# Moving the gates' bias product behind the expert loop, and pacing nine expert weight loads from GpSimd, in a one-core graph layer

## The chip, the cores and the metric

One core of one Trainium2 chip runs the whole layer as a single hand-ordered program: five engines with a program each, and semaphores between them. The metric is the device time of that core in microseconds, the median of several runs. The profile is of one further execution, whose own time is given beside it.

## The reference, cut to what matters

1250 nodes of 512 features pass through a graph convolution, an attention-like mixer and then a layer of 16 experts, of which each node uses its two best. Only the last part is touched by the change:

```python
logits = xt @ router_w.T + router_b
probs = softmax(logits)
topk_p, topk_i = top_k(probs, 2)
gates = sum(one_hot(topk_i) * topk_p)          # 1250 x 16
for e in range(16):
    h = gelu(xt @ w1[e].T + b1[e])             # 512 -> 256
    y = h @ w2[e].T + b2[e]                    # 256 -> 512
    out += y * gates[:, e]
x = x + out
```

The second bias is separable: the sum over the experts of gate times b2 is one product, gates (1250 x 16) by b2 (16 x 512). The kernel computes it so.

## The kernel before, in words

The nodes are cut into 10 tiles of 128 rows (the last has 98). FC_TILES groups them into 3, 3, 2 and 2. For each group the kernel makes the graph part's hidden and output products, normalises, and routes. Routing gives each (node, choice) a row ("slot") in a DRAM table `xs`, where every expert owns its own stretch.

What follows the last group, in order:

- GpSimd scatters the normalised rows into `xs`: 20 indirect DMAs, two per tile (L569). The last four belong to the last group and can start only when its slots are known (`slots_ready`).
- VectorE works out the tile table (`te`, `lies_at`, `tbase`, `npair`: which expert and which rows each 128-row tile of slots has) and then raises `route_ready`.
- ScalarE issues eight expert weight loads back to back (experts 1 to 8, L695) as soon as the last output product (`mix_ps`) is done. Each is 1 MB: 128 rows of 8 KB. SyncE has loaded experts 0 and 15 long before, and loads 9, 10, 11 just before the last routing.
- TensorE turns the gates of every tile (L1303, into bank 0 or 1), ScalarE copies them out (L700, `gt_saved`), TensorE multiplies them by b2 (L1309, into bank 2 or 3, `gb_ps`), and VectorE adds the result to `xr` (L1016, `gb_added`). Product t waits for the addition of t-2, since there are two banks.
- SyncE waits for all scatters (L400) and loads the first two tiles of slots, `xg[0]` and `xg[1]` (L402). TensorE turns them (`turn_rows`, L1315), ScalarE copies them (L704). SyncE then loads tiles 2 and 3 (L405), and the last three experts 12, 13, 14.
- The expert loop handles two tiles per turn. TensorE: first products (L1333), turning of the next two tiles (L1315), second products (L1346). ScalarE: Gelu (L714) and copies of turned rows (L720). VectorE copies the next tile's first weights into `w1_now` (L1026, after `w_ready` has counted its expert), and results out of PSUM (L1038). SyncE stores the results (L417) and loads the next slots (L414). TensorE reads the turn count and four table entries into registers (L1323, L1325, L1326) before each turn's first product (L1333).
- GpSimd counts the experts in order into `w_ready` (L575), and after the loop gathers both results of each node (L585). VectorE adds them with their gates (L1043, L1045), and SyncE stores the output (L422).

The order of instructions on an engine is the order of the text; a wait holds back everything behind it on its engine.

Of the kernel before, what the change touches and what calls it, by code (L numbers as in the profile page):

```python
# [23 lines left out]
P = 128  # L24
N = 1250
D = 512
NT = 10
# [6 lines left out]
FC_TILES = [range(0, 3), range(3, 6), range(6, 8), range(8, 10)]  # L34
# [20 lines left out]
EXP = 16  # L55
DFF = 256
KF = DFF // P
EW = KD * DFF + KF * D
# [10 lines left out]
def layer(nc, x, src, dst, wqkv, wo, bo, gw1, gb1, gw2, gb2, geps, rw, rb, ew, eb1, eb2, out):  # L69
    f32r = mybir.dt.float32r  # L70
    f32, f16, bf16, i32 = mybir.dt.float32, mybir.dt.float16, mybir.dt.bfloat16, mybir.dt.int32
    ALU = mybir.AluOpType
# [5 lines left out]
    with ExitStack() as ctx:  # L78
# [10 lines left out]
        arena = sb("arena", [P, SLAB // 4])  # L89
# [75 lines left out]
        xr = at(VT + NT * D * 4, [NT, D])  # L165
# [18 lines left out]
        logits, prob, tmp, oh1, oh2, rank, gates = (small(k, NT, EXP) for k in range(7))  # L184
# [7 lines left out]
        gates_t = at(S + 14336, [NT * P], parts=EXP)  # L192
        w1_now = at(S + 19456, [2, KD * DFF])

        ident = sb("ident", [P, P])
# [25 lines left out]
        b2_sb = sb("b2_sb", [EXP, D])  # L221
# [15 lines left out]
        bank = [ctx.enter_context(nc.psum_tensor(f"bank{i}", [P, 512], f32)) for i in range(8)]  # L237
# [8 lines left out]
        ew_in = [sem(f"ew_in{e}") for e in range(EXP)]  # L246
# [24 lines left out]
        mix_ps, x2_ready = sem("mix_ps"), sem("x2_ready")  # L271
# [19 lines left out]
        def rows(t):  # L291
            return LAST if t == NT - 1 else P
# [48 lines left out]
        def _(sp):  # L341
# [37 lines left out]
            def expert(e):  # L379
                sp.dma_start(arena[:, expert_at(e):expert_at(e) + EW], ew[e]).then_inc(ew_in[e], 16)  # L380
# [23 lines left out]
                sp.wait_ge(xgt_ps[a], 1)  # L404
                sp.dma_start(xg[:, a, :], rows_of(2 + a)).then_inc(xg_in[a], 16)  # L405

            for e in (12, 13, 14):
                expert(e)
            n = sp.value_load(npair[0:1, 0:1], min_val=1, max_val=(MAXT - 3) // 2)
            with sp.Fori(0, n) as j:  # L410
                for a in range(2):
# [14 lines left out]
        def _(pool):  # L426
# [139 lines left out]
            for t in range(NT):  # L566
                pool.wait_ge(slots_ready, 1 + sum(1 for tiles in FC_TILES if tiles[-1] < t))
                for k in range(2):
                    pool.indirect_dma_start(  # L569
                        out=xs, out_offset=bass.IndirectOffsetOnAxis(ap=slot[0:rows(t), k, t:t + 1], axis=0),  # L570
                        in_=x2n[0:rows(t), t, :], in_offset=None).then_inc(scattered, 16)

            for e in range(EXP):
                pool.wait_ge(ew_in[e], 16)
                pool.sem_inc(w_ready, 1)  # L575

            pool.wait_ge(route_ready, 1)
            n = pool.value_load(npair[0:1, 0:1], min_val=1, max_val=(MAXT - 3) // 2)
# [12 lines left out]
        def _(act):  # L591
# [99 lines left out]
                    act.activation(x2n_t[:, t % 2, :, :], bank[6][:, :].rearrange("p (k n) -> p k n", k=KD),  # L691
                                   copy).then_inc(x2nt_saved, 1)
            act.wait_ge(mix_ps, NT)
            for e in range(1, 9):
                act.dma_start(arena[:, expert_at(e):expert_at(e) + EW], ew[e]).then_inc(ew_in[e], 16)  # L695
            exponents(len(FC_TILES) - 1)

            for t in range(NT):
                act.wait_ge(gt_ps, t + 1)
                act.activation(gates_t[:, t * P:(t + 1) * P], bank[t % 2][0:EXP, 0:P], copy).then_inc(gt_saved, 1)  # L700

            for a in range(2):
                act.wait_ge(xgt_ps[a], 1)
                act.activation(xg_t[:, a, :, :], bank[4 + a][:, :].rearrange("p (k n) -> p k n", k=KD),  # L704
                               copy).then_inc(xgt_saved[a], 1)
            act.wait_ge(eb1_in, 16)
            act.wait_ge(route_ready, 1)
            n = act.value_load(npair[0:1, 0:1], min_val=1, max_val=(MAXT - 3) // 2)
# [15 lines left out]
        def _(dve):  # L724
# [285 lines left out]
            dve.sem_inc(route_ready, 1)  # L1010
            weigh(len(FC_TILES) - 1)

            for t in range(NT):
                r = rows(t)
                dve.wait_ge(gb_ps, t + 1)
                dve.tensor_tensor(xr[0:r, t, :], xr[0:r, t, :], bank[2 + t % 2][0:r, :], ALU.add).then_inc(gb_added, 1)  # L1016


            for a in range(2):
                dve.sem_inc(y_saved[a], 1)  # L1020
                dve.sem_inc(y_stored[a], 16)
# [17 lines left out]

            for t in range(NT):  # L1040
                r = rows(t)
                dve.wait_ge(yg_in[t], 32)
                link(dve.scalar_tensor_tensor(out=xr[0:r, t, :], in0=yg[0:r, 0, t, :], scalar=gate[0:r, 0, t:t + 1],  # L1043
                                              in1=xr[0:r, t, :], op0=ALU.mult, op1=ALU.add))
                dve.scalar_tensor_tensor(out=xr[0:r, t, :], in0=yg[0:r, 1, t, :], scalar=gate[0:r, 1, t:t + 1],  # L1045
                                         in1=xr[0:r, t, :], op0=ALU.mult, op1=ALU.add).then_inc(res_ready, 1)

        @block.tensor
        def _(pe):
# [244 lines left out]
            route(NT - 1)  # L1294
            ranks(len(FC_TILES) - 1)

            pe.wait_ge(b2_in, 16)
            for f, tiles in enumerate(FC_TILES):
                pe.wait_ge(gates_ready, f + 1)
                for t in tiles:  # L1300
                    if t >= 2:
                        pe.wait_ge(gt_saved, t - 1)
                    pe.transpose(bank[t % 2][0:EXP, 0:P], gates[:, t, :], ident[:, :]).then_inc(gt_ps, 1)  # L1303
                for t in tiles:
                    r = rows(t)
                    pe.wait_ge(gt_saved, t + 1)
                    if t >= 2:
                        pe.wait_ge(gb_added, t - 1)
                    pe.matmul(bank[2 + t % 2][0:r, :], gates_t[:, t * P:t * P + r], b2_sb[:, :],  # L1309
                              start=True, stop=True).then_inc(gb_ps, 1)  # L1310


            def turn_rows(a):
                for k in range(KD):
                    ins = pe.transpose(bank[4 + a][:, k * P:(k + 1) * P], xg[:, a, k * P:(k + 1) * P], ident[:, :])  # L1315
                ins.then_inc(xgt_ps[a], 1)

            pe.wait_ge(x2_ready, NT)
            for a in range(2):
                pe.wait_ge(xg_in[a], 16)  # L1320
                turn_rows(a)
            pe.wait_ge(route_ready, 1)
            n = pe.value_load(npair[0:1, 0:1], min_val=1, max_val=(MAXT - 3) // 2)  # L1323
            with pe.Fori(0, n) as j:
                e = [pe.value_load(te[0:1, bass.ds(2 * j + a, 1)], min_val=0, max_val=EXP - 1) for a in range(2)]  # L1325
                lies = [pe.value_load(lies_at[0:1, bass.ds(2 * j + a, 1)], min_val=expert_at(EXP - 1),  # L1326
                                      max_val=expert_at(0)) for a in range(2)]
                for a in range(2):
                    pe.wait_ge(w1_ready[a], j + 1)
                    pe.wait_ge(xgt_saved[a], j + 1)  # L1330
                    for m in range(KF):
                        for k in range(KD):
                            ins = pe.matmul(bank[a][:, m * P:(m + 1) * P],  # L1333
                                            w1_now[:, a, k * DFF + m * P:k * DFF + m * P + P],
                                            xg_t[:, a, k, :], start=(k == 0), stop=(k == KD - 1),
                                            skip_group_check=True)
                    ins.then_inc(h_ps[a], 1)
                for a in range(2):
                    pe.wait_ge(xg_in[a], 16 * (j + 2))
                    turn_rows(a)  # L1340
                for a in range(2):
                    pe.wait_ge(w_ready, e[a] + 1)
                    pe.wait_ge(hg_ready[a], j + 1)
                    pe.wait_ge(y_saved[a], j + 1)
                    for k in range(KF):
                        ins = pe.matmul(bank[6 + a][:, :], hg_t[:, a, k, :],  # L1346
                                        arena[:, bass.ds(lies[a] + KD * DFF + k * D, D)],
                                        start=(k == 0), stop=(k == KF - 1))
                    ins.then_inc(y_ps[a], 1)


# [29 lines left out]
```

## Time and profile before

| | |
|---|---|
| median of 3 runs | 878.91 us (877.94 to 879.23) |
| profiled execution, its own time | 879.67 us |
| span of the profile | 877.5 us |
| TensorE matmul busy | 775.1 us (88%) |
| VectorE, ScalarE, GpSimd busy | 521.7, 281.1, 155.3 us |
| mean granted TensorE clock | 0.942 |

Times in the rows are microseconds from the span's start. The granted clock is given as a share of full speed: 1.00 is 2.4 GHz and 0.50 is 1.2 GHz. "PEld" is TensorE's weight load, "SPq", "ACTq", "PEldq" the instruction sequencer of an engine. The work around the change lies between 676 us (last output product) and the end.

### The profile page before, as it was taken

The page shows a single profiled execution, that of the slowest core. Times are in us where ns is not written, and L with a number is a line of the kernel's source. Part 1 is how long each engine was busy: PE and PEld are TensorE (multiplying, and loading weights), DVE is VectorE, ACT ScalarE, POOL GpSimd, SP SyncE. Part 2 cuts the span into 40 slices and gives each one's busy share as a digit, 9 for nine tenths or more (in the row PEclk, how much of TensorE's full clock was granted, in tenths as well). Part 3 has the DMA queues.
Part 4 walks back from the last instruction along what each step waited for, and adds up shares of the span by engine and source line. Part 5 has one row for each costly group of instructions (what it writes and reads, how often), then busy time and mean ns, then how long its engine had stood idle before and what let it go on. Part 6 is the DMA issues. An engine that isn't in the chain of part 4 may idle for free.

```text
span 877.5 us, 11469 instructions
## 1 busy us (share of the span) xinstructions
PE 775.1 (88%) x3351; PEld 517.9 (59%) x3352; DVE 521.7 (59%) x1494; ACT 281.1 (32%) x578; POOL 155.3 (18%) x198
## 2 busy tenths in 40 slices
PE   4999998989989998979799999999998599999910
PEld 2555443666756676656577744677887256766700
DVE  4563336798989989898877534435445523333234
ACT  2212111352534444343345402323333123434300
POOL 5040003022130403040400042002021100000045
PEclk9999999999999999999799999999999559999965
DMA  9126000807162526253351091001015945343357
GB/s 296 8 44 241 1 0 1 295 1 251 46 210 87 182 104 198 98 160 137 105 191 49 1 357 47 1 0 72 1 73 192 377 184 187 109 135 114 131 163 235
DMA packets 48071, 111.61 MB, mean 127 GB/s; under 512 B 7066, under 2 KB 7082, under 8 KB 45584
## 3 DMA queue, kind: packets, MB, share of 16 engines
q1 hardware_dynamic: 43248, 91.41, 30.8%
q0 software_dynamic: 3616, 11.17, 4.0%
q10 hardware_dynamic: 1152, 8.39, 2.4%
q8 instruction: 24, 0.39, 0.2%
q14 instruction: 31, 0.25, 0.1%
HBM read 44.73 MB, written 58.54 MB: 118 GB/s over the span
## 4 chain that ended last, share of the span: by engine, by line
PE 70%; DVE 20%; issue 4%; POOL 2%; DMA 2%; ACT 2%; SPq 0%; DVEq 0%; POOLq 0%
PE bank L1110 8%; PE bank L1141 7%; PE bank L1272 7%; DVE arena L825 6%; PE bank L1218 6%; PE bank L1333 6%; PE bank L1169 6%; DVE p_lo L861 6%; PE bank L1346 5%; PE bank L1081 4%; PE bank L1152 4%; PE bank L1203 4%; DVE arena L827 3%; PE bank L1188 3%; PE bank L1185 3%
## 5 line engine op out<-in xcount | busy, mean ns | idle before, releaser
L657 ACT ACTIVATE p_hi<-bank 128x416 fp32r<-128x416 f32 (+1 forms) x240 | 123.8, 518 | 201.2 <-PE bank L1169 199.7
L861 DVE SCALAR_TENSOR_TENSOR p_lo<-bank,p_hi 128x416 fp32r<-128x416 f32 (+1 forms) x240 | 140.2, 586 | 40.7 <-ACT p_hi L657 39.7
L825 DVE TENSOR_SCALAR arena<-iota,arena 125x128 f16<-125x128 f16 x392 | 137.9, 352 | 37.0 <-PE bank L1081 34.8
L827 DVE TENSOR_SCALAR arena<-iota,arena 125x320 f16<-125x320 f16 x392 | 115.7, 295 | 0.0
L1169 PE MATMUL bank<-q_hi,k_hl 128*128 128x416 f32 (+1 forms) x240 | 114.9, 479 | 0.1
L1188 PE MATMUL bank<-p_lo,v_hl 128*128 128x416 f32 (+1 forms) x240 | 91.0, 379 | 21.6 <-DVE p_lo L861 21.2
L1110 PE MATMUL bank<-arena 128*128 128x512 f32 x200 | 103.0, 597 | 0.8 <-ACT arena L618 0.8
L1081 PE MATMUL bank<-arena 125*128 125x320 f16 x392 | 96.7, 311 | 5.8 <-issue 3.5
L1185 PE MATMUL bank<-p_hi,v_hl 128*128 128x416 f32 (+1 forms) x240 | 86.5, 360 | 0.0
L1169 PE MATMUL bank<-q_lo,k_hl 128*128 128x416 f32 (+1 forms) x240 | 86.1, 359 | 0.0
L1081 PEld LDWEIGHTS bank<-arena 125*128 125x128 f16 x392 | 34.4, 100 | 75.7 <-issue 53.2
L1141 PE MATMUL bank<-arena 128*128 128x416 f32 (+1 forms) x192 | 73.1, 529 | 2.1 <-ACT arena L600 2.1
L1272 PE MATMUL bank<-arena 128*128 128x384 f32 (+2 forms) x256 | 70.3, 430 | 0.0
L1188 PEld LDWEIGHTS bank<-p_lo,v_hl 128*128 128x128 f32 x240 | 46.6, 194 | 35.2 <-DVE p_lo L861 34.1
L1333 PEld LDWEIGHTS bank<-arena 128*128 128x128 f32 x448 | 53.0, 198 | 17.4 <-issue 16.0
L1333 PE MATMUL bank<-arena 128*128 128x128 f32 x448 | 55.3, 283 | 6.6 <-issue 5.6
L1026 DVE COPY arena<-arena 128x1024 f32 x30 | 20.8, 695 | 67.3 <-issue 67.3
L1169 PEld LDWEIGHTS bank<-q_hi,k_hl 128*128 128x128 f32 x240 | 47.1, 196 | 20.2 <-issue 13.5
L1272 PEld LDWEIGHTS bank<-arena 128*128 128x128 f32 x256 | 47.7, 190 | 17.6 <-issue 0.5
L1141 PEld LDWEIGHTS bank<-arena 128*128 128x128 f32 x192 | 36.2, 195 | 29.7 <-issue 26.3
L509 POOL COPY arena<-arena 125x20 f32 (+1 forms) x40 | 8.5, 212 | 246.8 <-DVE arena L827 207.5
L1346 PE MATMUL bank<-arena 128*128 x112 | 50.4, 592 | 0.0
(208 smaller groups left out, 1018.9 us busy)
## 6 DMA issues: line engine op xcount, KB each, us to landing
slots<-arena SPq DMA_DIRECT2D x6, 5376.0 KB, 19.3
slots<-arena SPq DMA_DIRECT2D x2, 5120.0 KB, 19.0
arena<-in_ew SPq DMA_DIRECT2D x8, 1024.0 KB, 10.7
arena<-in_ew ACTq DMA_DIRECT2D x8, 1024.0 KB, 13.2
arena<-slots SPq DMA_DIRECT2D x32, 256.0 KB, 2.8
slots<-arena SPq DMA_DIRECT2D x28, 256.0 KB, 2.1
arena<-in_gw SPq DMA_DIRECT2D x2, 2048.0 KB, 16.7
arena<-in_wqkv SPq DMA_DIRECT2D x3, 1024.0 KB, 14.2
```

Source lines behind the costliest of these rows:

```text
L657: act.activation(p_hi[0:kt, s % NPB, 0:n], bank[s % NQB][0:kt, 0:n], ACT.Relu).then_inc(p_hi_ready, 1)
L825: dve.tensor_scalar(ring[:, at_slot:at_slot + P], iota16[0:CE, 0:P], window_cols[:, i % WBUF, 1, k:k + 1], None, ALU.is_equal)
L827: dve.tensor_scalar(ring[:, at_slot + P:at_slot + OHW], iota16[0:CE, :], window_cols[:, i % WBUF, 0, k:k + 1], None, ALU.is_equal).then_in ...
L861: dve.scalar_tensor_tensor(out=p_lo[0:kt, s % NPB, 0:n], in0=bank[s % NQB][0:kt, 0:n], scalar=0.0, in1=p_hi[0:kt, s % NPB, 0:n].bitcast(f3 ...
L1081: return pe.matmul(bank[AW[w % 2]][:, 0:WCOL], of[:, at_slot:at_slot + P], of[:, at_slot + P:at_slot + OHW], start=start, stop=stop, skip_ ...
L1110: ins = pe.matmul(bank[NB][:, :], a_t[:, g % 2, t, :], xn[:, t, :], start=(t == 0), stop=(t == NT - 1))
L1141: ins = pe.matmul(bank[g % 5][:, 0:n], w_qkv[:, k, c:c + P], xn_t[:, k, o:o + n], start=(k == 0), stop=(k == KD - 1))
L1169: ins = pe.matmul(bank[s % NQB][0:kt, 0:n], k_hl[h % 2][:, t * P:t * P + kt], q[h % 2][:, o:o + n], start=first, stop=not first)
L1185: pe.matmul(bank[AV + m % 2][:, 0:n], v_hl[0:kt, t, h, :, :], p_hi[0:kt, s % NPB, 0:n], start=(t == 0), stop=False)
L1188: pe.matmul(bank[AV + m % 2][:, 0:n], v_hl[0:kt, t, h, :, :], p_lo[0:kt, s % NPB, 0:n], start=False, stop=(t == NT - 1)).then_inc(av_step, 1)
L1272: ins = pe.matmul(bank[g % 4][:, 0:n], w1[:, k, m * P:(m + 1) * P], rst_t[:, k, o:o + n], start=(k == 0), stop=(k == KD - 1))
L1333: ins = pe.matmul(bank[a][:, m * P:(m + 1) * P], w1_now[:, a, k * DFF + m * P:k * DFF + m * P + P], xg_t[:, a, k, :], start=(k == 0), stop ...
```

## The change

It has three parts, and it keeps what is computed.

1. The ten gate-by-bias products move behind the expert loop on TensorE, and the ten additions into the tail on VectorE, one ahead of each tile's two final additions. The turning of the gates stays before the loop: eight tiles ahead of `turn_rows`, the last two behind it; TensorE then waits until all ten are copied.
2. ScalarE issues only experts 1 and 2; SyncE no longer issues 12, 13 and 14.
3. GpSimd, after the scatters, waits until `xg[1]` has landed, and then issues 3, 4, 5, 6, 7, 8, 12, 13, 14: two at first and one more each time the next expert from number 3 on has been counted.

```diff
-            for e in (12, 13, 14):          # SyncE, after the loads of tiles 2 and 3
-                expert(e)
...
+            pool.wait_ge(xg_in[1], 16)      # GpSimd, after the scatters
+            pool.wait_ge(mix_ps, NT)
+            late = [3, 4, 5, 6, 7, 8, 12, 13, 14]
+
+            def load_next():
+                e = late.pop(0)
+                pool.dma_start(arena[:, expert_at(e):expert_at(e) + EW], ew[e]).then_inc(ew_in[e], 16)
+
+            load_next()
+            load_next()
             for e in range(EXP):
                 pool.wait_ge(ew_in[e], 16)
                 pool.sem_inc(w_ready, 1)
+                if e >= 3 and late:
+                    load_next()
...
-            for e in range(1, 9):           # ScalarE
+            for e in range(1, 3):
                 act.dma_start(arena[:, expert_at(e):expert_at(e) + EW], ew[e]).then_inc(ew_in[e], 16)
...
-            for t in range(NT):             # VectorE, before the loop
-                r = rows(t)
-                dve.wait_ge(gb_ps, t + 1)
-                dve.tensor_tensor(xr[0:r, t, :], xr[0:r, t, :], bank[2 + t % 2][0:r, :], ALU.add).then_inc(gb_added, 1)
...
             for t in range(NT):             # VectorE, after the loop
                 r = rows(t)
+                dve.wait_ge(gb_ps, t + 1)
+                link(dve.tensor_tensor(xr[0:r, t, :], xr[0:r, t, :], bank[2 + t % 2][0:r, :], ALU.add))
+                dve.sem_inc(gb_added, 1)
                 dve.wait_ge(yg_in[t], 32)
...
+            for f in range(len(FC_TILES) - 1):      # TensorE, before the loop
+                turn_gates(f)
             pe.wait_ge(x2_ready, NT)
             for a in range(2):
                 pe.wait_ge(xg_in[a], 16)
                 turn_rows(a)
+            turn_gates(len(FC_TILES) - 1)
+            pe.wait_ge(gt_saved, NT)
             pe.wait_ge(route_ready, 1)
...
+            pe.wait_ge(b2_in, 16)           # TensorE, after the loop
+            for t in range(NT):
+                r = rows(t)
+                if t >= 2:
+                    pe.wait_ge(gb_added, t - 1)
+                pe.matmul(bank[2 + t % 2][0:r, :], gates_t[:, t * P:t * P + r], b2_sb[:, :],
+                          start=True, stop=True).then_inc(gb_ps, 1)
```

(The words behind # in the diff name the engine; they are not in the code.) ScalarE's copies follow TensorE's order: gates of tiles 0 to 7, both `xg` copies, gates of tiles 8 and 9.

## Rows read from the trace of the kernel before

**Rows 1.** Busy time of each engine by stretch, with granted clock and DMA.
```profile
core 0: us, PE busy (x) PEld busy (x) DVE busy (x) ACT busy (x) POOL busy (x), PEclk, DMA share, GB/s
686.00:696.00 10.00, 4.91 (x15) 1.57 (x15) 8.45 (x33) 0.90 (x4) 4.38 (x4) 0.50 1.01 410
696.00:705.00 9.00, 8.43 (x12) 2.56 (x13) 2.96 (x6) 0.74 (x3) 0.00 (x0) 0.50 1.01 420
718.00:724.00 6.00, 6.00 (x38) 5.57 (x38) 0.82 (x2) 3.30 (x7) 0.00 (x0) 0.77 0.98 374
```

**Rows 2.** The chain that ended last, from routing into the loop: start, us, what.
```profile
693.94 0.12 DVE tbase L1008
...
710.05 3.79 PE bank L1309 x4
...
716.74 5.74 PE bank L1333 x32
...
727.41 3.81 PE bank L1333 x32
```

**Rows 3.** Instructions in order of time, last scatter to first loop turn.
```profile
692.21 1.32 POOL L569 DMA_INDIRECT slots<-arena,slot  x1 [0.30 <-issue]
...
709.42 0.69 DVE L1016 TENSOR_TENSOR arena<-arena,bank 128x512 f32<-128x512 f32 x1 [1.02 <-PE bank L1309]
709.73 0.48 ACT L700 ACTIVATE arena<-bank 16x128 f32<-16x128 f32 x2 [3.97 <-PE bank L1303]
...
713.76 1.97 PE L1315 MATMUL bank<-ident,arena 128*128 128x128 f32 x8
...
714.91 0.60 ACT L704 ACTIVATE arena<-bank 128x512 f32<-128x512 f32 x1 [4.70 <-PE bank L1315]
```

**Rows 4.** Single lines: the wait for the scatters, and landing times (L695, L402, L405).
```profile
L400 SPq EVENT_SEMAPHORE  x1: 17/17/17, 701.3 to 701.3; - x1
...
L695 ACTq DMA_DIRECT2D arena<-in_ew x8: 393/468/738, 680.4 to 684.1; - x8
...
DMA to landing us min/median/max: 5.1/13.2/21.5
...
L402 SPq DMA_DIRECT2D arena<-slots x2: 343/350/357, 702.4 to 703.5; - x2
...
DMA to landing us min/median/max: 3.6/3.8/3.9
...
DMA to landing us min/median/max: 2.8/2.8/2.8
```

**Rows 5.** Single lines: what TensorE's sequencer does between its last wait and the first turn.
```profile
L1323 PEldq TENSOR_LOAD <-npair x1: 307/307/307, 710.4 to 710.4; - x1
...
L1329 PEldq ALU_OP  x14: 32/32/32, 714.2 to 829.6; - x14
```

**Rows 6.** Single lines: landing of loop loads (L414), loop stores (L417), gathers (L585).
```profile
DMA to landing us min/median/max: 2.5/2.7/5.9
...
DMA to landing us min/median/max: 2.0/2.1/4.3
...
DMA to landing us min/median/max: 3.3/4.1/5.0
```

**Rows 7.** Instructions in order of time: GpSimd's first plain loads, at the span's start.
```profile
2.92 0.76 POOL L441 DMA_DIRECT2D arena<-in_dst  x1 [0.73 <-POOL ident L438]
```

**Rows 8.** Instructions in order of time: an addition beside a scatter, and the tail.
```profile
643.02 0.96 POOL L569 DMA_INDIRECT slots<-arena,slot  x1 [0.30 <-issue]
...
643.31 0.69 DVE L976 TENSOR_TENSOR arena<-arena,bank 128x512 f32<-128x512 f32 x1 [0.96 <-PE bank L1218]
...
847.45 0.75 DVE L1043 SCALAR_TENSOR_TENSOR arena<-arena,gate 128x512 f32<-128x512 f32 x1 [8.78 <-DMA arena<-slots,slot]
...
850.58 1.42 POOL L585 DMA_INDIRECT arena<-slots,slot  x1 [0.30 <-issue]
...
873.27 0.75 DVE L1043 SCALAR_TENSOR_TENSOR arena<-arena,gate 98x512 f32<-98x512 f32 x1 [1.26 <-DMA arena<-slots,slot]
```

More of the change, by code:

```diff
@@ L693, in _ @@
             act.wait_ge(mix_ps, NT)
-            for e in range(1, 9):
+            for e in range(1, 3):
                 act.dma_start(arena[:, expert_at(e):expert_at(e) + EW], ew[e]).then_inc(ew_in[e], 16)
             exponents(len(FC_TILES) - 1)
-            for t in range(NT):
-                act.wait_ge(gt_ps, t + 1)
-                act.activation(gates_t[:, t * P:(t + 1) * P], bank[t % 2][0:EXP, 0:P], copy).then_inc(gt_saved, 1)
+            for tiles in FC_TILES[:-1]:
+                for t in tiles:
+                    act.wait_ge(gt_ps, t + 1)
+                    act.activation(gates_t[:, t * P:(t + 1) * P], bank[t % 2][0:EXP, 0:P], copy).then_inc(gt_saved, 1)
             for a in range(2):
@@ L705, in _ @@
                                copy).then_inc(xgt_saved[a], 1)
+            for t in FC_TILES[-1]:
+                act.wait_ge(gt_ps, t + 1)
+                act.activation(gates_t[:, t * P:(t + 1) * P], bank[t % 2][0:EXP, 0:P], copy).then_inc(gt_saved, 1)
             act.wait_ge(eb1_in, 16)
@@ L1011, in _ @@
             weigh(len(FC_TILES) - 1)
-            for t in range(NT):
-                r = rows(t)
-                dve.wait_ge(gb_ps, t + 1)
-                dve.tensor_tensor(xr[0:r, t, :], xr[0:r, t, :], bank[2 + t % 2][0:r, :], ALU.add).then_inc(gb_added, 1)
             for a in range(2):
@@ L1295, in _ @@
             ranks(len(FC_TILES) - 1)
[L1297 to L1310, printed above, removed]
             def turn_rows(a):
@@ L1316, in turn_rows, with turn_gates @@
                 ins.then_inc(xgt_ps[a], 1)
+            def turn_gates(f):
+                pe.wait_ge(gates_ready, f + 1)
+                for t in FC_TILES[f]:
+                    if t >= 2:
+                        pe.wait_ge(gt_saved, t - 1)
+                    pe.transpose(bank[t % 2][0:EXP, 0:P], gates[:, t, :], ident[:, :]).then_inc(gt_ps, 1)
+            for f in range(len(FC_TILES) - 1):
+                turn_gates(f)
             pe.wait_ge(x2_ready, NT)
@@ L1349, in _ @@
                     ins.then_inc(y_ps[a], 1)
+            pe.wait_ge(b2_in, 16)
+            for t in range(NT):
+                r = rows(t)
+                if t >= 2:
+                    pe.wait_ge(gb_added, t - 1)
+                pe.matmul(bank[2 + t % 2][0:r, :], gates_t[:, t * P:t * P + r], b2_sb[:, :],
+                          start=True, stop=True).then_inc(gb_ps, 1)
 def kernel(x, src, dst, L0_gnn_W1, L0_gnn_b1, L0_gnn_W2, L0_gnn_b2, L0_gnn_eps, L0_mix_W_qkv, L0_mix_W_out,
```

## The prediction

> **What bounds the kernel now.** I read the chain of waits first, then busy time by stretch, then single lines. The reader should look only at what lies between the end of routing and the first turn of the expert loop. The tile table is ready at 694.1 (693.94 + 0.12) [rows 2], and the loop's first product starts at 716.74 [rows 2]: 22.7 us in which the chain is nearly all L1309, the gate-by-bias products, with L1303 and L1016 between them. They run at a granted clock of 0.50 (1.2 GHz) [rows 1].
>
> A second path runs beside this one and is shorter. From 686 to 705 the DMA engines are full (share 1.01, 410 to 420 GB/s) [rows 1]: that is ScalarE's eight weight loads, issued from 680.4 to 684.1 and landing up to 21.5 us later [rows 4]. The last scatter is issued at 692.21 [rows 3], but the wait for all scatters ends only at 701.3 [rows 4], and the two slot loads go out at 702.4 and 703.5 and take 3.6 to 3.9 us [rows 4]. So the second tile has landed at about 703.5 + 3.6 = 707.1. Taking the products away alone would leave this path; the change attacks both.
>
> **Part 1, the products leave.** Ten products, ten additions and their waits go from the stretch 695.5 to 713.8. Nothing needs them before the tail. What is late next is `xg[1]`.
>
> **Part 2, the scatters and slot loads meet empty DMA engines.** Only experts 1 and 2 are in flight from 680.4, 2 MB, which at the smallest landing time of such a load, 5.1 us [rows 4], are gone by 687. The last scatter starts at about 692.1 as now (it hangs on `slots_ready`, not on DMA). It then needs 3.3 to 5.0 us to land, by the gathers of the same engine and size [rows 6], the nearest rows; I take 4.0, so 696.1. Now it takes 701.3 - 692.2 = 9.1. SyncE needs 1.1 us from the wait to its first load (701.3 to 702.4) and 1.1 more to the second [rows 4]: issue at 698.3. A load of this kind with little beside it takes 2.8 us (the lower of the two landings of slot loads) [rows 4]. `xg[1]` lands at 701.1, between 700.4 and 702.1.
>
> Here a row shows how queues share. Four scatters, 1.05 MB in 2 KB rows, start at 688.2 and are all landed at 701.3 [rows 4], that is 80 GB/s, while the total is 410 to 420 [rows 1]. That is 2 parts in 10, as 2 KB stand to 2 + 8 KB. The Trainium skill says in "DMA: Bandwidth & Descriptors", section "Queues, rings and completion order", that each DMA engine goes round the rings that have work, a packet of descriptors at a time. By that rule the trace agrees (80 of 420); if the queues were served first come, first served instead, the scatters would have had to wait for nearly all of the loads, to about 684.1 + 21.5 = 705.6 [rows 4].
>
> **From `xg[1]` to the first product.** TensorE turns the tile: half of 1.97 us [rows 3], 1.0. ScalarE starts 0.15 later and copies it in 0.60, then copies the gates of tiles 8 and 9 in 0.48 [rows 3]. With 0.2 for hand-overs, `gt_saved` is complete at 701.1 + 0.1 + 1.0 + 0.15 + 0.6 + 0.5 + 0.1 = 703.55. This wait is new, and behind it on TensorE stand the reads of `npair`, two entries of `te` and two of `lies_at` into registers. Now they start at 710.4, right after the addition of 709.42 + 0.69 that releases the last product's wait, and end at 714.2 [rows 3, 5]: 3.9 us, hidden today under products and turnings that TensorE still had queued. With the change nothing covers them. The first product starts at about 703.55 + 3.95 = 707.5.
>
> The other inputs are earlier. GpSimd, which before counted `w_ready` freely, now waits for `xg[1]`, then issues two loads. Its plain loads take 0.76 us or less [rows 7], so it counts at about 702.7, and VectorE's copy (L1026) ends at 703.6. The queued work behind GpSimd's wait is only this counting. It stays 3.9 us clear of TensorE.
>
> The start moves from 716.74 to 707.5: -9.2 us (-10.8 to -8.0 by the ends above and half a microsecond of hand-overs).
>
> **Part 3, the first turn.** Its 32 products take 5.74 us against 3.81 in the next turn [rows 2], because the clock stands at 0.50 until about 720.8 (from the mean of 0.77 over 718 to 724) [rows 1], 4 us after the first product. Before the change TensorE was busy right up to it; now it idles 5 us. At the low level throughout, 32 products take 2 x 3.81 = 7.62: the bounds are 0 and +1.9, I take +0.7.
>
> **Part 4, weights beside the loop.** Nine loads, 9.4 MB, now go at the loop's start instead of six before it and three at it. The loop's own DMAs are 256 KB each: two loads (2.7 us) and two stores (2.1 us) per turn [rows 6], all on SyncE's queue. At the 80 GB/s found above, each takes 3.3 us and they queue. Loads issued about 1.2 us after the turning are needed 7.2 us later (a turn is 8.5 us). Two in a row take about 1.5 + 6.6 = 8.1, so up to 1 us late per turn. At the weights' share of 340 GB/s plus gaps they stream from 702 to about 731, which covers turns 0, 1 and most of 2. Turn 0's loads are issued at 702 and are in time. So 0.6 us in all, between 0 (landings grew only to 5.9 under today's three loads, and no turn was longer for it) [rows 6] and 4 (each of three turns stretched by the full excess of 12 us of SyncE transfers over 8.5, less the stores' slack). A late store is absorbed, since its buffer is wanted a turn later.
>
> Do weights come in time? The reference's own routing gives the 16 experts 2, 1, 1, 1, 3, 1, 3, 1, 4, 2, 1, 2, 1, 1, 1, 2 tiles (27, 14 turns). Experts 3 and 4 are first wanted in turn 1, before 727; 5 and 6 in turn 3, before 744; 7 and 8 in turn 5, before 761; 12 and 13 in turn 10. Two loads of 1 MB at 300 to 400 GB/s take 5 to 8 us, so the pairs land at about 709, 716 and 724: nothing waits.
>
> **Part 5, the tail.** The products run as soon as the loop ends, with the gathers' 9 us ahead of them. The gathers pace the tail: 873.27 - 847.45 over nine tiles is 2.87 us each [rows 8]. VectorE needs two operations of 0.75 and now one of 0.69, 2.3 with links, so it fits and only its idle time goes. Does the addition slow GpSimd's issue? One gather is 1.42 long beside a final addition of two SBUF operands, while a scatter beside an addition out of PSUM stayed at 0.96 [rows 8]. The moved one is of the latter kind. I take +0.3; the bounds are 0 and 10 x 0.25 = +2.5 (if each costs half of the excess of 1.42 over 0.95), and a gain is excluded since nothing leaves the tail.
>
> **The sum.** -9.2 + 0.7 + 0.6 + 0.3 = -7.6. The span goes from 877.5 to 869.9, the profiled execution from 879.67 to 872.1. The median lies 0.8 below that execution, so 871.3 us. ScalarE's shorter issue and SyncE's missing three loads cost and give nothing: both wait afterwards.
>
> **The rivals.**
> - *Register reads run ahead* (8%): the start is set by `gt_saved` and the copy, at 703.6. Then 3.9 less: 867.4. Against it: the reads stand behind the wait, and now they began right after the last one was released [rows 5].
> - *The loop pays* (17%): two or three turns stretched by 1 to 2 us each, and the clock at its worst end: about 875.5. The share of 80 in 420 speaks for it; today's turns beside three loads speak against it, but those were on SyncE's own queue.
> - *The scatters stay slow* (7%): the 9.1 us are theirs and not the loads'. `xg[1]` still lands at 707.1, the start is 713.5, -3.2 + 1.6: 877.3. The full DMA share of rows 1 speaks against it.
> - *GpSimd's queue starves the loop* (7%), the case on the other side. Experts 7 and 8 must have landed by 761, 60 us after the first issue, so a pair may take 20 us, 105 GB/s. Below this VectorE waits in `take_w1`; at 93 GB/s the whole gain is gone (three pairs 67.6 us). Rows have the queue at 80 under full DMA, and at about 183 in the gathers (0.52 MB per 2.87 us) [rows 8]. At 80, three pairs take 79 us: +19, so about 890. The Trainium skill warns in "SBUF — State Buffer", its box on the "DVE blocks DMA" trap, that GpSimd can't write descriptors while VectorE copies fp32 from SBUF to SBUF, which L1026 does twice a turn. No row of before shows a plain load of GpSimd's beside such a copy; that is why this case keeps 7%.
>
> **How the numbers follow.** The forecast has 56%, its own range 868.5 to 874.5; 5% are left for what I don't see, on either side. The range is to hold 8 in 10: from 867 (the register rival) to 877 (most of the rest but the starving one). Differences within 0.2% (1.8 us) count as no change, about what a measurement can tell here. Faster by more: forecast, register rival, loop pays and a little, 0.82. The same: half of slow scatters and tails, 0.08. Slower: starving and a part of the unseen, 0.10.
>
> **What would show it.** In the trace after: L400 released near 696; `xg[1]` landed near 701; TensorE's reads between 703.5 and 707.5 with the engine idle, the first L1333 at 707.5 and 5.7 to 7.6 long; turns 1 and 2 not above 9.5 us and the later ones at 8.5; gathers still 2.9 us apart with L1016's successor between them. It is wrong if L1026 waits on a weight load, if L400 is released after 699, or if the turns beside the loads reach 10 us or more.

## The result and the profile after

The changed kernel takes 868.85 us (median of 4 runs, 867.1 to 870.63) against 878.42 for the kernel before on the same chip: a ratio of 0.989, 95% interval 0.9863 to 0.9918. That is 9.6 us less, where 7.6 were forecast. The profiled execution took 867.1 us with a span of 865.3 (877.5 before).

Line numbers move with the edit: the first products are L1338 (L1333 before), the turning of slots L1309 (L1315), the scatters L567, the late weight loads L577, the read of the turn count L1328 (L1323), the bias products L1361.

The chain of waits of the changed kernel from the last scatter into the loop (start, us, what), to be held against [rows 2]:

```profile
690.42 0.30 issue
690.73 3.33 DMA slots<-arena,slot
...
694.08 0.02 SPq L400
...
696.25 2.92 DMA arena<-slots
...
699.21 1.13 PE bank L1309 x4
...
700.36 0.45 ACT arena L714
...
701.27 4.03 issue
705.30 5.47 PE bank L1338 x32
...
715.51 3.81 PE bank L1338 x32
...
724.07 3.81 PE bank L1338 x32
```

The bias products are gone from the chain. In their place stand the scatter's landing, the slot load, one turning, one copy, and 4.03 us of "issue": the profile's word for time in which TensorE waits for nothing that it shows. It is the register reads, whose rows on TensorE's sequencer are these (the read of the turn count, and the end of the address arithmetic of each turn, first and last start):

```profile
L1328 PEldq TENSOR_LOAD <-npair x1: 307/307/307, 701.3 to 701.3; - x1
...
L1334 PEldq ALU_OP  x14: 32/32/32, 705.1 to 817.6; - x14
```

The chain before had one more link, just ahead of its first product:

```profile
713.87 0.04 DVE arena L1016
...
714.26 0.55 DVEq L1023
...
715.99 0.70 DVE arena L1026
```

VectorE came last there: its last addition (L1016) starts at 713.87, its own register reads (L1023 and on) stand behind that, and its copy of the first weights (L1026) releases TensorE at 716.74. Of the 22.7 us from the tile table to the first product, in the prediction "nearly all L1309", the bias products hold 15.0, and these last 2.9 are VectorE's. They went with the additions: after the change this copy (now L1033) ends at 700.7, 4.6 us before the first product.

Busy time of each engine in the stretches of [rows 1] (columns as there):

```profile
686.00:696.00 10.00, 1.80 (x6) 0.44 (x5) 7.19 (x28) 1.58 (x7) 4.38 (x4) 0.50 0.27 93
696.00:705.00 9.00, 2.63 (x10) 1.69 (x10) 1.39 (x2) 1.50 (x4) 1.40 (x2) 0.50 0.70 239
705.00:714.00 9.00, 8.70 (x46) 7.36 (x47) 1.88 (x3) 3.40 (x7) 1.59 (x3) 0.79 0.99 376
718.00:724.00 6.00, 5.63 (x28) 3.37 (x27) 2.08 (x3) 3.05 (x7) 1.38 (x3) 1.00 1.00 371
```

The DMA share over the scatters falls from 1.01 to 0.27, and the full stretch now lies beside the first loop turns, at 371 to 376 GB/s.

**Where the 12.2 us of span went.** The last scatter is a good zero, because it hangs on routing alone. From its issue to the first product it is 24.5 us before (692.21 to 716.74, rows 2 and 3) and 14.6 after (690.73 to 705.30): 10.0 us. The first turn took 10.67 us before (716.74 to 727.41) and takes 10.21: 0.5. The other turns and the tail give 0.3 together. The remaining 1.5 lie ahead of the last scatter, where little was changed (six of ScalarE's weight issues and the first bias products are gone). Over the fourteen profiles of this study that instruction starts anywhere between 689.5 and 692.4, without order by kernel; so 1.5 of the 12.2 is the difference of two executions, and the medians (9.6) are the better measure.

### The profile page after: what moved, and what is told of

It reads as the page before. It is cut to its first block, busy times and chain, and to the rows that moved or that the text cites. A ratio compares the mean times of both kernels' runs of the same rounds, so it can differ in the third digit from the quotient of the medians.

```text
span 865.3 us, 11472 instructions
## 1 busy us (share of the span) xinstructions
PE 774.0 (89%) x3351; PEld 516.5 (60%) x3352; DVE 521.5 (60%) x1494; ACT 281.2 (33%) x578; POOL 160.4 (19%) x207
## 4 chain that ended last, share of the span: by engine, by line
PE 68%; DVE 17%; issue 6%; DMA 3%; POOL 3%; ACT 1%; SPq 1%; POOLq 0%; ACTq 0%; DVEq 0%
PE bank L1120 9%; PE bank L1282 7%; PE bank L1151 7%; PE bank L1338 6%; DVE arena L838 6%; PE bank L1179 6%; PE bank L1351 6%; PE bank L1228 5%; DVE p_lo L874 5%; PE bank L1091 4%; PE bank L1162 4%; PE bank L1213 4%; PE bank L1198 4%; DVE arena L840 3%; PE bank L1195 3%
## 5 line engine op out<-in xcount | busy, mean ns | idle before, releaser
L838 DVE TENSOR_SCALAR arena<-iota,arena 125x128 f16<-125x128 f16 x392 | 139.8, 357 | 37.0 <-PE bank L1091 34.8
L840 DVE TENSOR_SCALAR arena<-iota,arena 125x320 f16<-125x320 f16 x392 | 117.8, 301 | 0.0
L1033 DVE COPY arena<-arena 128x1024 f32 x30 | 20.8, 694 | 74.2 <-issue 68.1
L1338 PEld LDWEIGHTS bank<-arena 128*128 128x128 f32 x448 | 52.7, 197 | 20.7 <-issue 20.7
L1338 PE MATMUL bank<-arena 128*128 128x128 f32 x448 | 55.0, 282 | 9.9 <-issue 9.9
```

Of the source, the lines that this page charges most:

```text
L838: dve.tensor_scalar(ring[:, at_slot:at_slot + P], iota16[0:CE, 0:P], window_cols[:, i % WBUF, 1, k:k + 1], None, ALU.is_equal)
L840: dve.tensor_scalar(ring[:, at_slot + P:at_slot + OHW], iota16[0:CE, :], window_cols[:, i % WBUF, 0, k:k + 1], None, ALU.is_equal).then_in ...
L1338: ins = pe.matmul(bank[a][:, m * P:(m + 1) * P], w1_now[:, a, k * DFF + m * P:k * DFF + m * P + P], xg_t[:, a, k, :], start=(k == 0), stop ...
```

## The experiments

Two theories stood against each other at first. **Two paths**: the bias products and the scatters' wait ran side by side, and only taking away both pays; what then bounds the start is the serial tail of it, above all the register reads. **One path**: one of the two edits does it, the other is a bystander. Later runs ask what the loop pays for the weights that now flow beside it. "Turn" times are from the start of one turn's first product to the next, and "last scatter to first product" is read from the timeline of each kernel.

| kernel | median us | ratio to before (95%) | last scatter to first product | turns above 8.7 us |
|---|---|---|---|---|
| before | 878.42 | | 24.5 | 0: 10.67 |
| changed | 868.85 | 0.989 (0.9863 to 0.9918) | 14.6 | 0: 10.21 |
| after_again | 868.11 | 0.9893 (0.9868 to 0.9918) | 14.4 | 0: 10.34, 2: 9.65 |
| products_only | 873.6 | 0.9957 (0.9944 to 0.997) | 21.2 | 0: 10.31 |
| loads_only | 877.91 | 1.0005 (0.9991 to 1.0018) | 24.5 | 0: 10.35 |
| four_more_reads | 873.33 | 0.9947 (0.9931 to 0.9964) | 17.2 | 0: 10.65, 2: 9.88 |
| no_bias_product | 868.34 | 0.9886 (0.9869 to 0.9902) | 14.6 | 0: 10.4, 2: 9.45 |
| reads_first | 869.92 (of three) | 0.9911 (0.9877 to 0.9946) | 9.9 | 0: 13.64, 2: 12.05 |
| reads_first_no_late | 861.43 (of two) | 0.9811 (0.9791 to 0.983) | 9.5 | 0: 9.09 |
| reads_first_one | 868.48 | 0.9898 (0.9869 to 0.9928) | 9.7 | 0: 10.61, 5: 13.0 |
| reads_first_even | 865.16 | 0.9843 (0.9823 to 0.9863) | 9.6 | 0: 10.73 |
| nine_at_once | 871.67 | 0.9924 (0.9907 to 0.994) | 14.7 | 0: 10.23, 1: 12.73 |
| loads_on_sync | 878.9 | 1.0006 (0.9996 to 1.0015) | 14.5 | 0: 10.21, 1: 18.96 |
| turn_zero_free | 862.62 | 0.9824 (0.9805 to 0.9842) | 9.5 | 0: 9.09, 6: 9.63 |

The kernel before ran beside each group of kernels, with medians of 877.7 to 878.57; the ratios are to those.

**after_again.** No edit.

> The changed kernel once more, as the yardstick for the others, and for its own spread: its first four times lie in two pairs (867.1 and 867.4, 870.3 and 870.6), 3.2 us apart. Theory: the stretch from the last scatters to the loop's first product is 18.5 us in every execution, and what differs lies elsewhere; 867 to 871 us. Rival: the pairs differ in the changed stretch, by the clock of the first turn (5.5 us for its 32 first products in the first profile, up to 7.6 at 1.2 GHz throughout).

Measured: 867.5 to 868.95, between the two pairs, so the pairs were no two modes. The changed stretch repeats: 14.4 us against 14.6, first turn 10.34 against 10.21. What differs is ahead of it (the last scatter starts 0.9 us earlier) and one later turn of 9.65. Its chain shows why:

```profile
720.84 7.35 DMA arena<-slots
...
728.23 0.66 PE bank L1309 x4
```

A slot load issued at 720.84 takes 7.35 us beside two weight loads, and three towards its end (issued at 716.3, 721.6 and twice from 725.0), and TensorE waits for it. So the contention that I had priced at 0.6 us is there in one profile (turn 2 is 1.1 us longer) and not in the other.

**products_only.** The edit takes GpSimd's late loads out again (that part isn't shown) and puts the others back:

```diff
-            for e in range(1, 3):           # ScalarE
+            for e in range(1, 9):
                 act.dma_start(arena[:, expert_at(e):expert_at(e) + EW], ew[e]).then_inc(ew_in[e], 16)
...
+            for e in (12, 13, 14):          # SyncE, as before the change
+                expert(e)
```

> Part 1 alone: the ten bias products behind the loop, all weight loads as in the kernel before. Theory (two paths side by side, then the register reads): the wait for the scatters still takes 9.1 us from the last issue, xg[1] lands where it did before, and copies and reads (2.1 + 4.0 us) follow; the first product comes 3 to 4 us earlier than before, so a gain of 3 to 4 us against the kernel before, about 875 us. Rival (the products were the path, the loads a bystander): a gain of 9 us or more, as in the full change.

Measured: -4.1 us. In its chain the scatters land as late as before, and the same copy and the same reads follow them:

```profile
689.68 9.26 DMA slots<-arena,slot
...
699.99 3.86 DMA arena<-slots
...
706.87 4.01 issue
710.88 5.59 PE bank L1328 x32
```

**loads_only.** The reverse: the kernel before, with the paced loads from GpSimd and the bias products where they were.

```diff
-            for e in (12, 13, 14):          # SyncE
-                expert(e)
...
-            for e in range(1, 9):           # ScalarE
+            for e in range(1, 3):
...
+            load_next()                     # GpSimd, as in the change
+            load_next()
```

> Parts 2 and 3 alone: paced weight loads from GpSimd, the bias products still before the loop. Theory: the wait for the scatters ends about 3.4 us after the last issue instead of 9.1, but TensorE turns the slots only behind the products; the first product stays where it was, 878 us within 1. Rival (the loads held up more than the scatters): a gain above 2 us.

Measured: 877.91, ratio 1.0005. The slot loads now go out at 693.97, but TensorE works off its products first, and the slots lie ready behind them:

```profile
693.97 1.48 SPq L402 DMA_DIRECT2D arena<-slots  x2
...
696.82 5.49 PE L1319 MATMUL bank<-b_sb,arena 16*128 16x512 f32 x6
```

Alone the edits bring 4.1 and 0 us, together 9.6. That settles the two paths: 5.5 us exist only for the pair. Counted inside the traces, from the last scatter to the first product, it is 3.3 and 0 us alone and 10.0 together.

**four_more_reads.**

```diff
+            for _ in range(4):
+                pe.value_load(npair[0:1, 0:1], min_val=1, max_val=(MAXT - 3) // 2)
             n = pe.value_load(npair[0:1, 0:1], min_val=1, max_val=(MAXT - 3) // 2)
```

> The changed kernel with four more reads of the turn count on TensorE, just ahead of the real one and with their values unused. Theory (the reads stand bare on the path, 0.7 to 0.9 us each): the first product comes 2.8 to 3.6 us later after xg[1] has landed, 871 to 872 us. Rival (hidden behind another wait): 868.5.

Measured: the "issue" piece of the chain grows from 4.03 to 6.64 us, 0.65 for each read where 0.7 to 0.9 were expected, so they are serial and nothing covers them.

```profile
702.23 6.64 issue
```

The median rises by 5, more than the 2.6 of the reads. Of the 4.9 us by which its profile is longer than after_again's, 2.8 lie between the last scatter and the first product, 0.5 in turns 0 and 2 (10.65 + 9.88 against 10.34 + 9.65), and 1.9 ahead of the last scatter, where the kernels are the same (the rest of the kernel is 0.3 shorter). Ten executions should have evened out most of that, so about 2 of the 5 us stay open.

**no_bias_product.** The result lacks the sum of gates times the second biases: the ten products after the loop and the ten additions are left out.

```diff
-            pe.wait_ge(b2_in, 16)           # TensorE, after the loop: the ten products
...
-                dve.wait_ge(gb_ps, t + 1)
-                link(dve.tensor_tensor(xr[0:r, t, :], xr[0:r, t, :], bank[2 + t % 2][0:r, :], ALU.add))
-                dve.sem_inc(gb_added, 1)
```

> The changed kernel without the ten bias products and their additions in the tail; the term gates times b2 is left out of the result. Theory (the gathers pace the tail, and the moved work lies in VectorE's idle time): within 1 us of the changed kernel, 868. Rival (the additions slow the tail or GpSimd's issue): 1 to 3 us faster than the changed kernel.

Measured: 868.34 with ratio 0.9886, against 0.989 and 0.9893 for the changed kernel, with intervals of 1.5 to 2.5 us on either side. The moved work costs nothing that can be measured. In the changed kernel's timeline the addition (L1050) stands in VectorE's idle time between two gathers:

```profile
850.77 0.75 DVE L1053 SCALAR_TENSOR_TENSOR arena<-arena,gate 128x512 f32<-128x512 f32 x1 [0.87 <-DMA arena<-slots,slot]
851.56 0.75 DVE L1055 SCALAR_TENSOR_TENSOR arena<-arena,gate 128x512 f32<-128x512 f32 x1
...
852.23 0.68 DVE L1050 TENSOR_TENSOR arena<-arena,bank 128x512 f32<-128x512 f32 x1
...
861.10 0.75 DVE L1053 SCALAR_TENSOR_TENSOR arena<-arena,gate 98x512 f32<-98x512 f32 x1 [0.92 <-DMA arena<-slots,slot]
```

**reads_first.** All gates are turned first, and everything that can be read is read before the first wait for slots; the body of the loop is a function `one_turn`, called once for turn 0 and then in a loop from 1.

```diff
+            for f in range(len(FC_TILES)):
+                turn_gates(f)
+            pe.wait_ge(gt_saved, NT)
+            pe.wait_ge(route_ready, 1)
+            n = pe.value_load(npair[0:1, 0:1], min_val=1, max_val=(MAXT - 3) // 2)
+            e0, lies0 = entries(lambda a: slice(a, a + 1))
             pe.wait_ge(x2_ready, NT)
             for a in range(2):
                 pe.wait_ge(xg_in[a], 16)
                 turn_rows(a)
-            with pe.Fori(0, n) as j:
+            one_turn(0, e0, lies0)
+            with pe.Fori(1, n) as j:
```

> The changed kernel with TensorE's order altered: all gates are turned and copied, and the turn count and the first turn's four table entries are read into registers, before TensorE waits for the first slots; the first turn stands outside the loop for that. Theory (the reads are serial and bare, 4.0 us, and the copies of two gates before them 0.4): the first product starts about 4.5 us earlier than in the changed kernel, 1.6 us after xg[1] has landed, so 864 us. Rival (the reads only fill a wait for something else, such as GpSimd's counting or VectorE's copy): within 1 us of the changed kernel. One more loss may show: less of the first turn at the high clock, or turn 0 meeting its next slots late.

Measured: the theory's first half is right, and the time is worse. The first product comes 9.9 us after the last scatter instead of 14.6 (4.6 less, where 4.5 were expected); what releases it now is VectorE's first copy. But the median is 869.92. (It is that of three executions. The fourth took 4356 us and is outside the comparison; with it the median would be 870.45. I found no cause, and none of the 16 executions of the four later kernels with this order did the same.) The chain shows the loop's slot loads, where the changed kernel had products:

```profile
700.96 4.40 PE L1333 MATMUL bank<-arena 128*128 128x128 f32 x32 [0.35 <-DVE arena L1029]
```

```profile
702.07 6.90 DMA arena<-slots
...
709.01 1.12 PE bank L1305 x4
...
720.85 8.76 DMA arena<-slots
...
729.65 1.11 PE bank L1305 x4
```

(The first fence is a line of its timeline, the second its chain.) The 4 us of reads had hidden something: while TensorE read registers, the slots of tiles 2 and 3 were on their way beside the first weight loads. Started earlier, turn 0 waits for them.

**reads_first_no_late.** Every tile computes with expert 0's weights, so the result is another; the nine late loads are not issued.

```diff
-            load_next()
-            load_next()
             for e in range(EXP):
-                pool.wait_ge(ew_in[e], 16)
+                if e in (0, 1, 2, 9, 10, 11, 15):
+                    pool.wait_ge(ew_in[e], 16)
                 pool.sem_inc(w_ready, 1)
...
-            dve.tensor_scalar(lies_at[:, :], te[:, :], float(-EW), float(expert_at(0)), ALU.mult, ALU.add)
+            dve.tensor_scalar(lies_at[:, :], te[:, :], 0.0, float(expert_at(0)), ALU.mult, ALU.add)
```

> reads_first without the nine late weight loads; every tile computes with expert 0's weights, so the results are another's and only the time is of interest. Theory (reads_first lost its 4.3 us and more because its loop's slot loads share the DMA engines with the weights: turns 0 and 2 took 13.6 and 12.1 us, loads landed up to 8.8 us late): all turns but the first at 8.5 us, the first at 8.5 to 9.5 by the clock, and 861 to 862 us. Rival (the early start itself makes turns 0 and 2 long, by register reads or the order of the first turn): the two long turns stay, 868 to 870.

Measured: 861.43 in two executions, turn 0 at 9.09 and no other above 8.61. So the late weights cost reads_first 8.5 us; between the two profiles turn 0 differs by 4.6 and turn 2 by 3.5, 8.1 together. 861.4 is the floor for this order.

**reads_first_one.**

```diff
-            load_next()
             load_next()
             for e in range(EXP):
```

> reads_first with one late weight load in flight instead of two. Theory (between one load and the next the queues are free for a while, so a slot load lands within 6 us): turns 0 to 4 at 8.5 to 9.5, 863 us, which is below the changed kernel. Rival A (a share is a share: as long as weights flow the slot loads get 80 GB/s, now for longer): as reads_first, 870. Rival B (one at a time brings experts 3 and 4 too late, after 716): turn 1 waits for a copy of first weights, 866 or more.

Measured: 868.48, but for a reason that neither rival named. Turns 1 to 4 and all from 6 on take 8.4 to 8.6, as the theory says. Turn 5 takes 13.0. GpSimd's rows show why: its counting passes experts 8, 9, 10, 11 in one go, since the last three were loaded long ago, and each step issues one more load.

```profile
741.06 1.86 POOL L577 DMA_DIRECT2D arena<-in_ew  x3 [6.08 <-DMA arena<-in_ew]
```

```profile
744.04 9.53 DMA arena<-slots
```

Three loads in one burst, and the slot load issued behind them (second fence, the chain) takes 9.53 us. The changed kernel has the same step, one expert later: when 8 has landed, 13 and 14 go out together (its last two issues, from 723.1) while 12 is still in flight, so there it is not "two at a time" but three.

**reads_first_even.**

```diff
-                if e >= 3 and late:
+                if e in (3, 4, 5, 6, 7, 8, 12, 13):
                     load_next()
```

> reads_first_one with the late loads truly one at a time: in that kernel, as in the changed one, the step past the experts 9, 10, 11 (in long before) issues 12, 13 and 14 together, and its turn 5, with three loads in flight, took 13.0 us while all turns but the first took 8.5. Here 12 is issued when 8 has landed, 13 when 12 has, 14 when 13 has. Theory (what a turn loses goes by how many weight loads are in flight beside its slot loads): no turn above 9 us but the first, 863.5 to 865, below every version so far that computes all. Rival (the loss falls on some turn in any case, as the loads' phase against the turns drifts): one turn of 10 us or more again, 867 or more.

Measured: 865.16, ratio 0.9843 (0.9823 to 0.9863). The turn of 13 us is gone, and no turn but the first is above 8.6. Turn 0 still takes 10.73, held by a slot load of 6.10 us:

```profile
701.31 6.10 DMA arena<-slots
...
707.45 1.11 PE bank L1304 x8
```

**nine_at_once.**

```diff
-            load_next()
-            load_next()
+            for _ in range(9):
+                load_next()
```

> The changed kernel with all nine late loads issued together by GpSimd behind xg[1], no pacing. Theory (pacing matters because weights and slot loads share the engines; two in flight keep them nearly full already, nine do so without a gap): the loads of turns 0 to 2 land 8 to 12 us after issue, each of these turns 1 to 4 us longer, 871 to 875 us. Rival (the pacing buys nothing, two in flight are as bad as nine): within 1 us of the changed kernel.

Measured: 871.67, 3 us above the changed kernel. Of turns 0 to 2 only turn 1 is long (12.73), by this load:

```profile
713.33 9.58 DMA arena<-slots
...
722.96 1.11 PE bank L1307 x4
```

So pacing is worth about 3 us in the changed kernel's order. The expectation of several long turns was too dark: nine loads together, the last issued at 704.0, are through 24.4 us later, a fast end as well as a crowded one. They land one by one, about 3 us apart. Three had landed when the slot load above went out at 713.33, and two were left when it landed.

**loads_on_sync.**

```diff
+            for e in (3, 4, 5, 6, 7, 8, 12, 13, 14):    # SyncE, behind the loads of tiles 2 and 3
+                expert(e)
```

> The changed kernel with the nine late loads on SyncE's own queue, all issued behind the first four slot loads and ahead of the loop. Theory (one queue is served in order, so the loop's first slot loads wait behind 9 MB at about 400 GB/s, some 23 us, and then nothing is shared any more): turn 0's slot loads land near 726, turn 1 is about 8 us longer, the others 8.5, 875 to 878 us. Rival (the share per queue is the whole story and the own queue does not matter): as nine_at_once.

Measured: 878.9, the whole gain given back. Turn 1 takes 18.96 us, and the slot load behind the weights 15.61. It lands at 726.4, 0.7 us after the last of the nine, of which about six were still to land when it was issued:

```profile
710.75 15.61 DMA arena<-slots
...
726.41 1.97 PE bank L1299 x8
```

A queue of one's own is the larger part of why GpSimd's loads work: the slot loads then share, where on SyncE's queue they wait for all that is ahead of them.

**turn_zero_free.** On top of reads_first_even:

```diff
-            for e in range(1, 3):           # ScalarE: expert 3 as well
+            for e in range(1, 4):
...
+            for e in range(4):              # GpSimd counts 0 to 3 at once
+                pool.wait_ge(ew_in[e], 16)
+                pool.sem_inc(w_ready, 1)
-            pool.wait_ge(xg_in[1], 16)
+            pool.wait_ge(xg_in[0], 32)
+            pool.wait_ge(xg_in[1], 32)
...
+            late = [4, 5, 6, 7, 8, 12, 13, 14]
...
+            for e in range(4, EXP):
...
+                if e in (4, 5, 6, 7, 8, 12, 13):
                     load_next()
```

> reads_first_even with expert 3 loaded by ScalarE beside 1 and 2 (engines are idle there), experts 0 to 3 counted without a wait for slots, and the first late load issued only when the slots of tiles 2 and 3 have landed. In reads_first_even turn 0 took 10.73 us, its slot loads landing 5.0 and 6.1 us after issue beside the first late load; with no late load at all it took 9.09. Theory (the same sharing costs turn 0 its 1.6 us): turn 0 at 9.1 to 9.3, all others at 8.5 to 8.7, 863 to 864 us. Rival (the loss moves to turn 1, where expert 4 is now copied for tile 5 and its load began later): turn 1 above 9.5 us, total unchanged at 865.

Measured: 862.62, ratio 0.9824 (0.9805 to 0.9842). Turn 0 takes 9.09, exactly as with no late loads, and the slot loads of tiles 2 and 3 land in 2.7 us at most. One later turn (6) took 9.63 in the profile, against the 8.5 to 8.7 expected, and its chain waits for a slot load again:

```profile
749.08 7.30 DMA arena<-slots
```

Only one weight load was beside it, the last, issued at 749.33; the one before had landed at 748.7. So one load in flight makes such turns rarer and does not rule them out. This version beats the kernel before by 15.8 us (878.41 beside it) and the changed kernel by about 6, and is 1.2 above the floor of reads_first_no_late.

## Why the prediction was right, and where it was not

- **The two paths and the scatters** (-9.2 from the start of the loop). Right. From the last issue to the wait's end it took 3.35 us where I had 4.0; the two steps of SyncE 2.17 where I had 2.2; the slot load 2.96 (696.25 to 699.21) where I had 2.8; turning and copies 2.06 where I had 2.45; reads 4.03 where I had 3.95. The sum is 14.6 against 15.3, and -10.0 lies within the stated -10.8 to -8.0 (the ends and half microseconds that the prediction names add up to -10.4 to -7.7, so these bounds were not worked out right). products_only and loads_only show both halves: 4.1, 0, and 9.6 together. I had taken 4.0 for the scatter's landing from the median of the gathers; their smallest (3.3) was the better row, perhaps because a gather waits behind its neighbours and the last scatter no longer did; no run separates this. The rival "the scatters stay slow" falls: they were awaited at 694.1. The prediction did not see VectorE's 2.9 us at the end of the old chain, which cost its sum nothing, since it counted from the first product.
- **The reads come bare onto the path.** Right, and shown twice: four_more_reads (+0.65 each) and reads_first (4.6 us earlier). The rival "reads run ahead" falls.
- **The first turn** (+0.7). Wrong in sign. It took 10.21 us after, 10.67 before, and 10.2 to 10.4 in every profile with the 4 us pause (10.65 with the 6.6 us one of four_more_reads, 10.35 without one in loads_only). TensorE's pause cost nothing: the clock stood at 0.50 before and after, the 32 first products took 5.47 and 5.59 us in the two profiles of the changed kernel against 5.74 [rows 2], and by the mean clock of single microseconds the level rose 4.0 us into them before and 3.5 after. In reads_first, where the products follow the turning at once, it rose 1.2 us into them, and the same products took 4.40 us.
- **The weights beside the loop** (+0.6, bounds 0 and 4). The size is about right for this order: turn 2 took 8.5 in one profile and 9.65 in the other (above the 9.5 that the prediction had named as its sign), 9.88 and 9.45 in two kernels like it. The mechanism is shown by the slot loads' landing times: up to 3.1 us with no weight load beside them (2.7 for turn_zero_free's tiles 2 and 3), 2.5 to 6.1 with one in reads_first_even and 7.3 in turn_zero_free, 2.6 to 8.8 with two or three, 7.7 and 9.5 behind a burst of three, 7.6 and 9.6 after nine issued together. But I had not seen what carries the size. The changed kernel's own 4 us of reads hold turn 0 back until the slots are in; take them away and turn 0 loses 4.6 us to the weights. The 3.5 of reads_first's turn 2 come from a slot load of 8.76 us, where the same load took 5.2 and 7.35 in the two profiles of the changed kernel; why it was slower there is open. And I had read "two at a time" from the diff's loop without following it past experts 9 to 11, where three are in flight. One row behind the price was misread, too: the last two tiles have 128 and 98 rows, so the four scatters carry 0.93 MB and not 1.05, and their share of 420 GB/s was 71 and not 80.
- **The tail** (+0.3). Zero within what can be measured.
- **The starving queue**, the rival on the other side, did not come. GpSimd's loads took 5.1 to 9.4 us each, 6.8 in the median. The box of the Trainium skill that I put beside it ("SBUF — State Buffer", on the "DVE blocks DMA" trap) is borne out by these rows of reads_first: an issue beside VectorE's copy takes 0.74 us where one alone takes 0.53, and it ends 0.11 us after the copy. In reads_first_one and reads_first_even an issue that starts 0.14 us before the copy takes 0.95 and ends 0.12 after it. So the issue is held until the copy is over, but a copy lasts only 0.69 us: 0.2 to 0.4 us on a queue with tens to spare.

```profile
705.23 0.69 DVE L1029 COPY arena<-arena 128x1024 f32 x1 [2.89 <-POOLq L583]
705.29 0.74 POOL L577 DMA_DIRECT2D arena<-in_ew  x1 [4.27 <-DMA arena<-in_ew]
```

Without the 1.5 us ahead of the last scatter the profiled execution gained 10.7 where I had 7.6: 0.7 more from the start's sum, 1.2 from the first turn (0.7 forecast as loss, 0.5 come as gain), and 1.2 from the later turns and the tail (0.9 forecast as loss, 0.3 come as gain). The medians gained 9.6: that leaves out the 1.5, and other executions probably pay about 1 us in turn 2, as three of the four profiles with this order do. Every small term had been rounded to the dark side, so the measured 868.85 lies only 0.35 above the lower end of the forecast's own range, 868.5. The start's term carried the forecast; the first turn's had the wrong sign.

## What to carry to other kernels

When two stalls run side by side, cost the edits as a pair: here they brought 4.1 and 0 us alone and 9.6 together, and only what arrives last at the common wait counts. Before calling a removed stall a gain, list what its time was hiding, the sequencer's own work too: 4 us of register reads lay under the products, and turn 0's 4.6 us of DMA contention lay under the reads. Bulk loads beside a latency-bound loop belong on another queue, one in flight, started only when the loop's first small loads have landed; follow the pacing rule through the cases in which its condition is met at once. Even so paced, one slot load in turn_zero_free took 7.30 us.

## What the hardware showed that I had not expected

- The longest latency of a small load rises with what is in flight on the other queue, and most of the rise comes with the first load. A 256 KB load took 2.4 to 3.1 us with no 1 MB load beside it, up to 7.30 with one, up to 8.76 with two to three, and 9.53 behind a burst of three. After nine issued together it took 9.58, but by then six were left, and two at its end: no run shows it beside all nine. The ranges overlap (as little as 2.5 us with one, 2.6 with two), so the count alone does not fix a load's time.
- On one queue, the same load with about six of 1 MB still ahead of it took 15.61 us and landed 0.7 us after the last of them: there it waits in order.
- A plain load's issue on GpSimd that meets an fp32 copy of VectorE's ended 0.11 to 0.13 us after the copy in five profiles: it took 0.74 to 0.95 us instead of 0.53.
- A register read on TensorE's sequencer costs 0.65 us, and a turn's five of them with their arithmetic 4.0, as soon as a wait stands right ahead of them and the engine's queue has run dry.
- The part of the kernel ahead of the last scatter ended at times 2.6 us apart in five profiles whose kernels are the same up to there, and 2.9 apart over all fourteen. A single pair of profiles can't show a gain of 1 us at this place; an interval counted from a common event inside the trace (14.6, 14.4, 14.6, 14.7, 14.5 us in the five profiles with this order and these waits) can.
